# GpSimd waits for its last scattering additions before it leaves its part of the program

## The reference, cut to what matters

```
mod = silu(c) @ wmod                      # sa, ca, ga, sb, cb, gb; ga and gb bounded away from 0
h = layernorm(x) * (1 + ca) + sa
x = x + ga * attn(h)                      # RMS norm, causal conv, gated linear recurrence, gated MLP
h = layernorm(x) * (1 + cb) + sb
x = x + gb * ffn(h)

def ffn(tokens):                          # 8 experts, each token goes to its best 2
    probs = softmax(tokens @ gate_w); top_w, top_idx = top_k(probs, 2), normalised
    for e in range(8):
        out_e = gelu(tokens @ w1[e] + b1[e]) @ w2[e] + b2[e]     # 256 -> 1024 -> 256
        combined = combined + cw[:, e:e + 1] * out_e
    return combined + tokens
```

## Time and profile before

| what | before |
|---|---|
| median of three timed runs | 290.25 us (289.51 to 292.1) |
| span of the profiled execution, which is its own time | 290.3 us |
| mean granted TensorE clock | 0.970 |
| TensorE busy | 274.4 us (95%) |
| VectorE, ScalarE busy | 198.6 us (68%), 179.7 us (62%) |
| GpSimd busy | 121.5 us (42%) |
| data moved by DMA | 37.94 MB, mean 131 GB/s |

### The profile page before, as it was taken

One profiled execution on the slowest core, in us unless ns is written; L12 is line 12 of the kernel. 1 busy time (PEld: TensorE's weight loads), 2 busy tenths in 40 slices (PEclk: granted clock), 3 DMA queues, 4 the chain that ended last, 5 costly groups with the idle time before them and its releaser, 6 DMA issues.

```text
span 290.3 us, 4525 instructions
## 1 busy us (share of the span) xinstructions
PE 274.4 (95%) x1594; PEld 224.0 (77%) x1594; DVE 198.6 (68%) x465; ACT 179.7 (62%) x297; POOL 121.5 (42%) x99
## 2 busy tenths in 40 slices
PE   7989999999999999999999999999999999999980
PEld 2655555468697888776697888999999999999970
DVE  4489599749739759668777386876776768686520
ACT  4238787774495349926885238958769594949100
POOL 8032300000415014484683406548383838566661
PEclk9979999999999999999997599999999999999997
DMA  6990000000008563244179239639295775717133
GB/s 193 382 302 1 2 1 0 0 2 0 0 2 304 167 186 56 72 128 169 46 235 285 64 121 253 175 85 340 77 291 136 224 207 172 210 21 216 20 42 37
DMA packets 32374, 37.94 MB, mean 131 GB/s; under 512 B 7956, under 2 KB 27980, under 8 KB 32332
## 3 DMA queue, kind: packets, MB, share of 16 engines
q1 hardware_dynamic: 26736, 30.10, 32.7%
q0 software_dynamic: 4928, 7.44, 11.4%
q10 hardware_dynamic: 684, 0.06, 0.2%
HBM read 31.63 MB, written 8.90 MB: 140 GB/s over the span
## 4 chain that ended last, share of the span: by engine, by line
PE 70%; DVE 14%; ACT 5%; issue 4%; DMA 2%; POOL 2%; POOLq 1%; DVEq 0%; ACTq 0%
PE bank L1014 19%; PE bank L1043 15%; PE bank L686 8%; PE bank L611 6%; PE bank L783 5%; PE bank L876 2%; PE bank L995 2%; PE bank L1038 2%; PE bank L1037 2%; DVE u L1554 2%; PE bank L622 2%; PE bank L630 1%; DVE xhat L1457 1%; PE bank L640 1%; DMA x_tok<-in_L_attn_x 1%
## 5 line engine op out<-in xcount | busy, mean ns | idle before, releaser
L2065 POOL DMA_INDIRECT out_x<-y_tok,meta x24 | 49.1, 2047 | 46.7 <-DVE y_tok L1907 28.9
L1043 PE MATMUL bank<-w_hi,own 128*128 128x256 f32 x256 | 51.4, 296 | 0.0
L1043 PEld LDWEIGHTS bank<-w_hi,own 128*128 128x128 f32 x256 | 42.7, 200 | 2.3 <-issue 1.6
L1889 DVE TENSOR_TENSOR own<-own_raw,own 128x256 fp32r<-128x256 f32 x64 | 27.1, 424 | 21.0 <-ACT own L1370 16.5
L1014 PE MATMUL bank<-xe_hi,w_hi 128*128 128x320 f32 x128 | 40.1, 313 | 1.5 <-DVE xe_lo L1860 0.8
L1014 PE MATMUL bank<-xe_lo,w_hi 128*128 128x320 f32 x128 | 39.6, 309 | 0.0
L1014 PE MATMUL bank<-xe_hi,w_lo 128*128 128x320 f32 x128 | 39.5, 309 | 0.0
L1364 ACT ACTIVATE own_raw<-bank,b1c 128x320 f32<-128x320 f32 x64 | 33.9, 530 | 8.1 <-PE bank L1014 7.7
L1043 PE MATMUL bank<-w_lo,own 128*128 128x256 f32 x128 | 37.3, 291 | 0.0
L2055 POOL DMA_INDIRECT gb_rows<-gb_table,meta x24 | 24.4, 1015 | 11.7 <-issue 6.7
L1370 ACT ACTIVATE own<-own_raw 128x320 fp32r<-128x320 f32 x64 | 28.8, 462 | 0.0
(11 more groups left out here) (249 smaller groups left out, 626.0 us busy)
## 6 DMA issues: line engine op xcount, KB each, us to landing
e_raw<-in_L_ffn_w SPq DMA_DIRECT2D x16, 1024.0 KB
x_rows<-in_L_attn_x SPq DMA_DIRECT2D x1, 2560.0 KB
xe_tok<-x_rows SPq DMA_DIRECT2D x7, 256.0 KB
raw_m<-in_L_attn_up_W SPq DMA_DIRECT2D x2, 768.0 KB, 9.9
x_tok<-in_L_attn_x SPq DMA_DIRECT2D x2, 512.0 KB, 5.2
out_x<-x_tok SPq DMA_DIRECT2D x1, 1024.0 KB, 5.2
wmod<-in_L_wmod SPq DMA_DIRECT2D x1, 768.0 KB, 11.9
raw_m<-in_L_attn_down_W SPq DMA_DIRECT2D x1, 768.0 KB, 12.6
```

The costliest lines, as they stand in the source:

```text
L1043: ins = nc.tensor.matmul(bank[b][0:n, 0:D], l, r, start=(c == 0 and t == 0), stop=(c == KE - 1 and t == 2))
L1889: nc.vector.tensor_tensor(own_lo[e % 2][:, f, :], own_raw[:, f % 4, 0:whole], own_hi[e % 2][:, f, 0:whole].bitcast(F32), ALU.subtract)
L2065: nc.gpsimd.indirect_dma_start(out_rows, bass.IndirectOffsetOnAxis(ap=ids[0:n, e, k, E:E + 1], axis=0), y_tok[e % 2][0:n, k, :], None, com ...
```

## The change

```diff
@@ in GpSimd's program, first arm of the If @@
                 for e in range(E):
                     add_y(e)
                     if e + 2 < E:
                         gather_gb(e + 2)
+                for s in range(2):
+                    pool.wait_ge(y_added[s], 16 * ST * (E // 2))
             with pool.Else():
```

## The result

| | kernel before | changed kernel |
|---|---|---|
| median of six runs | 289.88 us (287.3 to 292.1) | 293.43 us (292.32 to 294.51) |
| ratio of the runs | 1 | 1.0158, 95% interval 1.0118 to 1.0198 |
| profiled execution: its span | 290.3 us | 292.3 us |
| profiled execution: its time | not listed beside it | 294.02 us |

The change makes the kernel slower. The forecast was 292.7 us and "within 1%". The median lies inside the stated range (287.0 to 293.8 us), but the ratio lies beyond 1%, and nearly twice as far out as the +0.85% of the prediction. Two things have to be explained: what the wait costs, and why the first comparison shows more than that. A ratio here leaves out the runs that lie more than 1.5% above the fastest of their kernel, which are called slow; where this text says "over all runs", none is left out.

What follows compares the result with a forecast made beforehand. TensorE bounds nearly all of the kernel, but GpSimd's last DRAIN sets the tail: 286.8 + 5.79 + 0.24 = 292.8 us, +2.5 us, so a median of 292.7 us (+0.85%), range 287.0 to 293.8 us.

Steps and rivals of the forecast that it cites:

- within 1%: Verdict on the whole time: +0.85% lies just inside what can't be told from no change; same 0.56, slower 0.26, faster 0.18.
- The sum of the tail: End of kernel: DRAIN start 286.8, plus walk 5.79, plus 0.24 gives 292.8 us against 290.3, +2.5 us.
- The DRAIN's work: GpSimd's last DRAIN: goes through all 70 DMAs after the engine's last instruction, 5.79 us, 83 ns each.
- The walk: GpSimd's last DRAIN: one-by-one pass over its issued DMAs, 5.79 us, held back behind the landing; likeliest case, chance 0.36.
- The release and the barrier: GpSimd's queue end: released with SyncE at 286.5 us, DRAIN from 286.8, span ending 0.24 us after the DRAIN.
- The short DRAIN: Rival at GpSimd's last DRAIN: with all landed it needs only 188 ns, median 287.15 us, -1.07%; chance 0.25.
- The fixed tail behind the landing: Rival at GpSimd's last DRAIN: fixed bookkeeping of at most 3.5 us after the last DMA lands, +0.2 us; chance 0.20.
- The whole 7.7 us: Rival at GpSimd's last DRAIN: its own work runs from its queue start, all 7.7 us, 294.7 us, +1.5%; chance 0.11.
- It does nothing: Rival at the new waits: conditions already hold when GpSimd gets there, time stays; excluded by SyncE's rows, no chance given.
- From the profiled execution to the median: Whole time: median 290.25 us is 0.05 us from the profiled 290.3 us span, so +2.5 us makes it 292.7.

Runs made afterwards that it cites:

- e6: Kernel before, without the wait, plus 24 DMAs of 1 KB issued early on GpSimd's queue: ratio 0.9994 (0.9933 to 1.0055).
- e3: Kernel before, no wait at the end, with seven GpSimd DRAINs in mid-program where it waits anyway: ratio 0.9892 (0.9836 to 0.9947).
- e4: Changed kernel, wait kept, with the same seven early GpSimd DRAINs as e3: ratio 0.9917 (0.9876 to 0.9957) to the kernel before.
- e10: Kernel before, no wait, with one early GpSimd DRAIN behind the first two gathers: ratio 0.9916 (0.988 to 0.9952).
- e1: Changed kernel measured again with no edit, against the kernel before: ratio 1.0071 (1.0018 to 1.0125).
- e7: Changed kernel measured a third time, on one chip with e8, against the kernel before: ratio 1.0112 (1.0039 to 1.0185).
- e8: Kernel before measured against itself, nothing changed: ratio 1.0047 (1.0003 to 1.0092).
- e2: Changed kernel with GpSimd waiting for the even experts' additions only, already landed, against the kernel before: ratio 0.9992 (0.9947 to 1.0036).

## Why the prediction was right and where it was wrong

The sum of the tail held, and what failed is the step behind it, from +2.5 us to what a timed comparison shows: that it "lies just inside" the 1% which can't be told from no change. The comparison showed +1.58%, with 1.18% as its lower end, and the two repeats also stand clear of 1. What the traces show is still 2.5 us. Where the rest of the first comparison comes from stays open in its rows, and the runs as a whole speak for scatter; both are taken up below.

**The DRAIN's work: right.** The step was "the DRAIN goes through all of them one by one, from the moment the engine has finished its last instruction", 5.79 us for 70 DMAs. It measured 5.785 us in three executions of the changed kernel; 94, 42 and 6 DMAs gave 7.8, 3.48 and 0.54 us. The 83 ns for each were 82. e6 shows the count as the cause, e3 and e4 that a DRAIN retires what it has gone over. The walk alone isn't the whole of it: a DRAIN with fewer DMAs is held by the landing as well (e3, e10), which with 70 doesn't come to bear.

**The release and the barrier: right.** GpSimd was released together with SyncE, its DRAIN started 0.3 us later (286.0 to 286.3), and the span ended 0.24 us behind the DRAIN. The term "+2.5 us" is what the tails show (10.1 against 7.6 us; 10.1 in e1 and in e7 too).

**The rivals.** The short DRAIN is ruled out: with nothing under way the DRAIN still took 5.785 us, not 0.19. The Trainium skill's rule about the full count (DMA: Bandwidth & Descriptors, "Why a DMA increments its semaphore by 16 and not by 1") holds, as nothing moved after it, but what GpSimd does behind it isn't a wait for data. The fixed tail behind the landing is ruled out by e3 and e6, with 0.3 and 5.3 us behind it. The whole 7.7 us are ruled out, since the work starts with the engine's end. "It does nothing" is ruled out by the wait's release at 286.0 us.

**From the profiled execution to the median: wrong.** The prediction took 290.3 us as the time of the profiled execution and set it beside the median of 290.25. In all runs with both numbers, the time is 1.69 to 1.90 us more than the span. So the profiled execution of the kernel before took about 292.1 us (an estimate, as its time isn't listed beside it): it is the slowest of the three runs shown, not their middle, and 290.3 us isn't "its own time". A difference of two tails survives this; the claim that execution and median agree within 0.05 us doesn't. The median of six runs was 289.88, and with 2.5 us more it would be 292.4 us, not the 293.43 measured.

**"Within 1%": wrong by the first comparison, and open in its size.** Its interval (1.18% to 1.98%) excludes 0.85%. Three comparisons of the same kernel gave 1.58, 0.71 and 1.12%. Over all runs their differences are 3.8, 2.0 and 2.3 us, in the mean 2.5 us when each is weighted by its 6, 12 and 6 runs of the changed kernel. All 24 runs of the changed kernel together have a mean of 292.8 us, all 93 of the kernel before 290.5 us: +2.3 us, with a standard error of 0.4. So the size of the term, 2.5 us, is borne out by time too, and a second cost isn't needed. The first comparison's own 3.8 us have a standard error of 0.8. Its six runs of the kernel before have a mean of 289.6 us, 0.8 to 1.0 us below that kernel in the three later comparisons; its six changed runs have 293.4 us, 0.5 to 1.1 us above the later ones. No row explains this surplus: ahead of the last landing its profile was 0.5 us earlier than that of before. What does differ is the execution. One kernel's times run from 286.74 to 293.28 us in 29 runs, and the last DMA instruction started at 282.71 us in one profile of the kernel before and at 279.23 in another. Two stretches of each of these two profiles show the clock in it (us, busy by engine, PEclk, DMA share, GB/s). The kernel before, first profile:

```profile
0.00:30.00 30.00, 26.45 (x114) 15.55 (x115) 19.96 (x64) 13.29 (x21) 11.48 (x21) 0.94 0.63 213
140.00:180.00 40.00, 38.54 (x205) 32.50 (x205) 26.62 (x53) 23.73 (x44) 19.60 (x17) 0.87 0.59 179
```

The same kernel in e8:

```profile
0.00:30.00 30.00, 26.69 (x106) 15.19 (x106) 18.77 (x62) 13.28 (x20) 9.70 (x21) 0.89 0.63 213
140.00:180.00 40.00, 38.42 (x236) 33.13 (x235) 30.77 (x64) 27.86 (x54) 23.05 (x19) 1.00 0.66 185
```

From 140 to 180 us the first had a granted clock of 0.87, part of that stretch at the lower of the two levels (1.2 GHz), and got through 205 matmuls; the second had 1.00 and got through 236. In the first 30 us it was the other way, 0.94 against 0.89. The two profiles differ by more than the effect, with the same kernel. That such differences alone make up the surplus of the first comparison is argued here, not shown.

## What to carry to other kernels

A DRAIN of GpSimd, also the one at the end of a block, goes over every DMA that GpSimd has issued since its last DRAIN, at 82 ns for each, also those that landed long ago, and it doesn't end before the last of them has landed. A wait for the last landing ahead of it cost 2.5 us here, since the walk can run while the last DMAs are in flight. It is better to put DRAINs where GpSimd is idle for longer than its last DMAs need to land, so that the last DRAIN finds few DMAs left. When the effect in question is under 1%, read it from the trace, from a point that both kernels have in common, since here the timed ratio of an unchanged kernel strayed by 0.5%.

## What the runs showed of the hardware that was not expected

- A DMA of 1 KB that landed 200 us ago costs GpSimd's last DRAIN as much as one of the others, most of which are indirect: 24 of them added 2.0 us (e6), and each of the 64 between e4 and the changed kernel 82 ns.
- Seven DRAINs in the middle of GpSimd's program took 3.4 us from the tail and left the last addition where it was (issued at 282.70 against 282.71 us), though one of them held the additions of expert 1 back by 0.3 us.
- A DRAIN that meets a DMA still under way ends a fixed time behind its landing, 0.28, 1.20 and 1.76 us for 6, 28 and 42 DMAs gone over (e3, e10): about half of its walk stays behind the landing.
- Of the two added waits only one has an instruction in the trace; the other, for the even experts, stands with the branch behind it, and in e2 it adds none.
- The device time is 1.7 to 1.9 us longer than the span from the first to the last instruction.
